# A windowed-attention block on one core: new order of stages, score weights of 49 columns, long matmuls in two 64-column halves, first MLP layer in f16

## The reference

```
xw   = windows of 7x7 pixels (64 per image), 49 tokens of 96 channels
xn   = layernorm(xw) * g + b
q,k,v = split(xn @ qkv_w.T + qkv_b)            # 12 heads of 8
attn = softmax(q * 8**-0.5 @ k.T + bias[head]) # 49 x 49
x1   = x + (attn @ v) @ proj_w.T + proj_b
c    = depthwise 3x3 convolution of x1, then batch norm (fixed statistics)
h    = gelu(c @ w1.T + b1)                     # 384 hidden channels, exact gelu
out  = c + (h @ w2.T + b2)
```

## Time and profile before

| | us |
|---|---|
| median of three runs | 3758.8 |
| lowest and highest | 3752.88, 3760.82 |
| the profiled execution | 3757.64 |
| its span, first to last instruction | 3755.8 |
| TensorE busy | 3535.0 (94%) |
| ScalarE busy | 3101.7 (83%) |
| VectorE busy | 2937.8 (78%) |
| GpSimd busy | 1133.5 (30%) |

### The profile page before, as it was taken

How to read it: one execution, slowest core, us unless ns; L and a number is a source line. 1 busy time by engine, 2 the same in 40 slices (tenths; PEclk the granted TensorE clock), 3 DMA queues, 4 the chain that set the end, 5 groups by cost and what they waited for, 6 DMA issues and landing times.

```text
span 3755.8 us, 189287 instructions
## 1 busy us (share of the span) xinstructions
PE 3535.0 (94%) x83724; PEld 2303.3 (61%) x83724; DVE 2937.8 (78%) x5155; ACT 3101.7 (83%) x5123; POOL 1133.5 (30%) x1550
## 2 busy tenths in 40 slices
PE   4999999999999999999999999999999999999998
PEld 2666666666666666666666666666666666666664
DVE  4778787877878778787877878787787878778786
ACT  2788888888888888888888888888888888888886
POOL 2232332323233232333233233232323323232332
PEclk9999999999999999999999999999999999999999
DMA  1232332323233232322323233232323223232321
GB/s 46 82 91 85 89 89 84 91 84 91 85 88 90 84 91 84 91 87 87 88 86 91 85 90 90 84 91 84 91 85 89 88 85 92 83 91 84 90 89 47
DMA packets 269476, 321.37 MB, mean 86 GB/s; under 512 B 55124, under 2 KB 252181, under 8 KB 268663
## 3 DMA queue, kind: packets, MB, share of 16 engines
q1 hardware_dynamic: 235894, 232.12, 21.6%
q0 software_dynamic: 32768, 77.14, 6.2%
HBM read 39.35 MB, written 38.54 MB: 21 GB/s over the span
## 4 chain that ended last, share of the span: by engine, by line
PE 76%; ACT 12%; DVE 7%; issue 4%; SPq 1%; DMA 0%; POOL 0%; POOLq 0%; DVEq 0%; ACTq 0%
PE a_ps L438 13%; PE sm_ps L322 10%; PE o_ps L339 8%; PE a_ps L357 6%; PE a_ps L430 6%; DVE mx L673 5%; PE st_ps L307 5%; PE d_ps L349 5%; PE b_ps L430 4%; PE d_ps L430 4%; ACT sq L561 4%; PE b_ps L280 4%; ACT sq L563 4%; ACT sq L557 3%; PE b_ps L282 2%
## 5 line engine op out<-in xcount | busy, mean ns | idle before, releaser
L695 DVE SCALAR_TENSOR_TENSOR s<-ximg,cols,s 96x392 f32<-96x392 f32 x2048 | 1260.0, 615 | 20.8 <-POOL s L597 2.9
L673 DVE TENSOR_REDUCE mx<-sm_ps 128x12 f16<-128x588 f32 x1024 | 780.9, 763 | 435.4 <-PE sm_ps L322 435.4
L597 POOL TENSOR_TENSOR s<-ximg,cols 96x392 f32<-96x392 f32 x256 | 215.6, 842 | 2384.7 <-DVE y L726 2384.7
L499 ACT ACTIVATE p<-st_ps 128x588 f32<-128x588 f32 x1024 | 669.5, 654 | 130.7 <-PE st_ps L307 126.6
L322 PEld LDWEIGHTS sm_ps<-k_all,q_all 127*64 127x64 f16 x24576 | 472.5, 113 | 315.6 <-issue 210.5
L438 PE MATMUL a_ps<-g,w_s 128*96 128x392 f32 x1536 | 602.2, 501 | 0.0
L604 POOL DMA_DIRECT2D ox<-o_sb x1024 | 580.8, 570 | 47.9 <-issue 31.8
L322 PE MATMUL sm_ps<-k_all,q_all 127*64 127x49 f16 x24576 | 580.5, 192 | 7.9 <-DMA q_all<-ql 6.4
L307 PEld LDWEIGHTS st_ps<-q_all,k_all 128*64 128x64 f16 x24576 | 476.1, 113 | 151.8 <-issue 147.9
L307 PE MATMUL st_ps<-q_all,k_all 128*64 128x49 f16 x24576 | 562.3, 191 | 0.0
L339 PE MATMUL o_ps<-p,v 128*32 128x49 f32 x24576 | 428.1, 211 | 131.0 <-DVE mx L673 129.5
(11 more groups left out here) (98 smaller groups left out, 5539.7 us busy)
## 6 DMA issues: line engine op xcount, KB each, us to landing
ox<-o_sb POOLq DMA_DIRECT2D x1024, 73.5 KB, 2.6
k_all<-kh SPq DMA_DIRECT2D x512, 96.0 KB
q_all<-qh SPq DMA_DIRECT2D x512, 96.0 KB
x_sb<-in_x SPq DMA_DIRECT2D x256, 147.0 KB, 2.4
out<-y SPq DMA_DIRECT2D x256, 147.0 KB, 2.9
k_all<-kl SPq DMA_DIRECT2D x256, 96.0 KB
q_all<-ql SPq DMA_DIRECT2D x256, 96.0 KB
q_all<-mxt SPq DMA_DIRECT2D x256, 12.0 KB, 2.0
```

Of the source, the lines that this page charges most:

```text
L499: af(p32[:, q, :, :].rearrange("p (b h) n -> p b h n", b=2), st_ps[:, :, 0:HALF].rearrange("p b (h n) -> p b h n", n=TOK), ACT.Exp).then_i ...
L673: v.tensor_reduce(mx[:, (st[1] - lag) % 2, :, p].rearrange("p (b h) -> p b h", b=2), sm_ps[:, :, 0:HALF].rearrange("p b (h n) -> p b h n", ...
L695: v.scalar_tensor_tensor(acc, image_rows(st, lag, k // 3, k % 3), cw_c[:, k:k + 1], acc, ALU.mult, ALU.add)\
```

## The change

It does the following.

- TensorE's long matmuls go through `wide`, which issues two matmuls with 64 columns of weights each, into partitions 0 to 63 and 64 to 127. The weights of `centred`, `variance`, `projection` and `second` are padded with zeros to 128 columns; those of queries and keys take the neighbouring columns. `values` does the same. The score matmuls take 49 columns of weights, not 64; the unused rows of the score banks are cleared once in the setup.
- The first MLP layer: w1 is split into two f16 parts (times 256), and s2 into sh (GpSimd, `image_high`) and sl (GpSimd, `image_low`), three f16 passes (`wide_three`), Gelu with scale 1/256.
- The values go to v32 in one VectorE multiplication (`values_out`) with a mask column, 128 x 768 elements, for both windows of a pair; ScalarE's half is gone.
- Each of four groups of scores, maxima, exps, value products, taps and hidden parts has a semaphore of its own, with one count per chunk. `free` lists who used a bank last.
- The banks are dealt anew: centred, the second layer and hidden 0 in b_ps; variance, queries, projection and hidden 2 in a_ps; keys, values and hidden 1 in d_ps.
- The order of a step and several lags are new on every engine, as the loops at the end of the diff's parts show. STEPS is 267.

```diff
-        x_in = sems("x_in", 4)
+        x_in = sems("x_in", 8)
...
+            for s in range(STEPS):
+                term(k_all, 2, kh, kh_done, s - 4)
+                term(q_all, 2, ql, ql_done, s - 4)
+                store(s - 11)
+                load(s)
+                maximum_row(s - 5)
+                first_term(k_all, 1, kl, kl_done, s - 3)
+                term(q_all, 0, qh, qh_done, s - 3)
+                term(k_all, 0, kh, kh_done, s - 3)
+                term(q_all, 1, qh, qh_done, s - 3)
...
+            def wide(o, w, m, start=True, stop=True):
+
+                for h in range(2):
+                    last = mm(o[64 * h:64 * h + 64], w[:, 64 * h:64 * h + 64], m, start=start, stop=stop)
+                return last
+
+            def wide_three(o, sh, sl, mh, ml):
+
+                wide(o, sh, mh, stop=False)
+                wide(o, sh, ml, start=False, stop=False)
+                return wide(o, sl, mh, start=False)
...
-                        last = mm(st_ps[64 * w:64 * w + 64, h // HH, c0:c0 + TOK], k_all[:, r, h, n:n + WP],
-                                  q_all[:, r, h, n:n + TOK], start=True, stop=True)
+                        last = mm(st_ps[64 * w:64 * w + TOK, h // HH, c0:c0 + TOK], k_all[:, r, h, n:n + TOK],
+                                  q_all[:, r, h, n:n + TOK], start=True, stop=True)
...
+                free(pe, (y_done, c-8), (g_done[0], c-8), (xn_done, c-1))
+                at = c % CPI * CT
+                wide(b_ps[0:128, 0:CT], center[:, :], x_sb[:, at:at + CT]).then_inc(xc_done, 1)
...
+                if k == 1:
+                    wait(pe, sl_done, c)
+                if k == 0:
+                    free(pe, (xn_done, c+7), (y_done, c-1), (g_done[0], c-1))
+                elif k == 1:
+                    free(pe, (v32_done, c+5), (kl_done, c+6), (g_done[1], c-1))
+                elif k == 2:
+                    free(pe, (sum_done, c+2), (lnv_done, c+7), (ql_done, c+6), (g_done[2], c-1))
+                wide_three(hidden_ps[k][:, 0:CT], w1_h[:, k * 128:(k + 1) * 128], w1_l[:, k * 128:(k + 1) * 128], sh[:, :], sl[:, :]).then_inc(hid_done[k], 1)
...
+            for s in range(STEPS):
+                max_scores(s - 2, 0)
+                hidden(s - 8, 2)
+                exp_scores(s - 4, 3)
+                values_times_p(s - 4, 0)
+                second(s - 8, 1)
+                max_scores(s - 2, 1)
+                keys(s - 1)
+                queries(s - 1)
+                second(s - 8, 0)
+                second(s - 8, 2)
+                exp_scores(s - 3, 0)
+                values_times_p(s - 4, 2)
+                values_times_p(s - 4, 3)
+                max_scores(s - 2, 2)
+                centred(s)
+                values(s - 2)
+                exp_scores(s - 3, 1)
+                variance(s)
+                max_scores(s - 2, 3)
+                exp_scores(s - 3, 2)
+                projection(s - 5)
+                values_times_p(s - 3, 1)
+                maxima_rows(s - 2)
+                hidden(s - 7, 1)
+                hidden(s - 7, 0)
...
+            for s in range(STEPS):
+                inverses(s - 5)
+                exp(s - 4, 3)
+                outputs(s - 4, 0)
+                query_high(s - 1)
+                exp(s - 3, 0)
+                outputs(s - 4, 1)
+                square(s)
+                exp(s - 3, 1)
+                log_variance(s)
+                root(s)
+                exp(s - 3, 2)
+                act.preload_act_table_set("gelu_and_others")
+                gelu(s - 7, 1)
+                input_high(s)
+                gelu(s - 7, 0)
+                gelu(s - 7, 2)
+                act.preload_act_table_set("natural_log_exp_and_others")
+                log_sums(s - 4)
+                key_high(s)
...
+            def image_high(c):
+
+                if not real(c):
+                    return
+                wait(pool, tap_done[8], c)
+                wait(pool, hid_done[2], c - 1)
+                pool.sem_inc(turn, 1)
+                nc.gpsimd.tensor_copy(sh[:, :], s2[0:C, c % 2, :]).then_inc(sh_done, 1)
...
+                tt(sl[:, :], s2[0:C, c % 2, :], sh[:, :], ALU.subtract).then_inc(sl_done, 1)
+
+            for s in range(STEPS):
+                image_high(s - 7)
+                image_low(s - 7)
+                first_tap(s - 6)
+                input_low(s)
+                to_channels(s - 3)
...
+                v.tensor_tensor(v32[:, c % 2, :, :, :].rearrange("p h n (d x) -> p (h n d) x", x=4)[:, :, 0:2],
+                                d_ps[:, 0:NP * C].unsqueeze(2).broadcast_to([128, NP * C, 2]),
+                                half_c[:, :].unsqueeze(1).broadcast_to([128, NP * C, 2]), ALU.mult).then_inc(v32_done, 1)
...
+            for s in range(STEPS):
+                tap(s - 7, 3)
+                tap(s - 7, 4)
+                tap(s - 7, 5)
+                maxima(s - 2, 1)
+                key_low(s - 1)
+                normalise(s - 5)
+                tap(s - 7, 6)
+                block_out(s - 8)
+                tap(s - 7, 7)
+                query_low(s - 1)
+                maxima(s - 2, 2)
+                tap(s - 7, 8)
+                values_out(s - 2)
+                maxima(s - 2, 3)
+                input_normal(s)
+                image_sum(s - 5)
+                maxima_out(s - 2)
+                tap(s - 6, 1)
+                tap(s - 6, 2)
+                maxima(s - 1, 0)
```

More of the change, by code:

```diff
@@ L269, in _, with load, term @@
-            run(sp, step)
+            def load(c):
+                if not real(c):
+                    return
+                wait(sp, sum_done, c - CPI)
+                at = c % CPI * CT
+                sp.dma_start(x_sb[:, at:at + CT], dram_rows(x, c)).then_inc(x_in[c % 8], 16)
+            def term(t, n, part, done, c):
+                if not real(c):
+                    return
+                wait(sp, done, c)
+                sp.dma_start(t[n:TERMS:4, c % 4, :, :], part[:, c % 2, :]).then_inc(exp_in[c % 4], 16)
@@ new lines, in first_term, with maximum_row @@
+            def first_term(t, n, part, done, c):
+                if real(c):
+                    wait(sp, sm_done[3], c - 4)
+                    wait(sp, st_done[3], c - 4)
+                    term(t, n, part, done, c)
+            def maximum_row(c):
+                if not real(c):
+                    return
+                wait(sp, mxt_out, c)
+                sp.dma_start(q_all[MAXROW:MAXROW + 1, c % 4, :, :].rearrange("p h (n c) -> p (h n) c", c=2 * WP),
+                             mxt[:, c % 2, :]).then_inc(row_in[c % 2], 16)
@@ L606, in _, with input_low, first_tap @@
-            run(pool, step)
+            def input_low(c):
+                if not real(c):
+                    return
+                wait(pool, xh_done, c)
+                tt(xl[0:C, c % 2, :, 0:TOK], xn[:, :, :], xh[0:C, c % 2, :, 0:TOK], ALU.subtract).then_inc(xl_done, 1)
+            def first_tap(c):
+                if not real(c):
+                    return
+                wait(pool, sum_done, c)
+                wait(pool, y_done, c - 2)
+                tt(s2[0:C, c % 2, :].rearrange("c (r q) -> c r q", q=SIDE), image_rows(c, 0, 0),
+                   cw_c[:, 0:1].unsqueeze(2).broadcast_to([C, WS, SIDE]), ALU.mult).then_inc(tap_done[0], 1)
@@ L777 @@
         low[row:row + n] = -1.0
+    half = np.zeros((128, 2), np.float32)
+    for w in range(2):
+        half[64 * w:64 * w + TOK, w] = 1 / UP
     col = lambda v: a(v).reshape(C, 1)
@@ L793 @@
         "eye": np.eye(128, dtype=np.float32),
-        "low": low,
+        "low": low, "half": half,
     }
```

664 lines of the change are left out of this document (279 added, 385 removed).

## The result

The changed kernel takes 3697.1 us (median of 4 runs, 3688.9 to 3708.0) beside 3756.7 for the kernel before: ratio 0.984, 95% interval 0.981 to 0.988. It is faster by 1.6%, where 3317 us (-11.7%) was forecast and the range ended at 3510. The executions profiled took 3757.6 us before and 3688.9 us after.

A forecast was written before the change was run, and what follows sets the result against it. TensorE bounded the old kernel; afterwards loops crossing engines would. The larger loop, 12.4 us, plus 0.1 for margins gives 12.5 per step; 248 x 12.5 + 215 + 2 = 3317 us, range 3170 to 3510.

The forecast's parts named there:

- the sum of 11.5 us: TensorE's work per step after the change, without waits, with halves running side by side: 11.5 us.
- no 0.09: Expected sign on TensorE: the 0.09 us per change of weight-column shape vanishes between scores and long layers.
- rival B: Crossing loops longer, by slower GpSimd or VectorE work, no 49-column gain, or late second halves: 13.1 us, 3466 us; chance 0.21.
- rival C: On TensorE, f32 halves run one after the other: 15.4 us per step, 4036 us, slower than before; chance 0.05.
- ScalarE and VectorE: Busy time per step on these engines: ScalarE 11.25 us with two table loads, VectorE 11.5 with values_out at 1.0.
- GpSimd: mechanism: GpSimd's four DMA issues stand before its copy (0.85 us) and remainder (1.3), delaying hidden 1 on TensorE by 0.8.
- Loop 2: Chain from TensorE through outputs, GpSimd's DMA issues, copy and remainder to hidden 1 and the next step: 12.3 us.
- The DMAs: this step: SP's six term transfers: last issued at 9.3 us, landed some 2.5 later, before the next step at 12.3.
- rival D: No gain in time: another wait, the six term DMAs above all, lands 1.8 us later; 14.27, 3757 us; chance 0.03.
- The third theory: From the experiments, not the prediction: several loops without slack turn any jitter into time; called the weaker one.

The follow-up runs named there:

- e11: Changed kernel with the transfer order of e5 and score groups of 12 matmuls with a doubled moving operand (odd heads get even heads' scores): 3297.1 us.
- e5: Changed kernel with its six term transfers in another order on SyncE, both transfers of kh first: 3562.6 us, ratio 0.948.
- e12: Changed kernel with the order of e5, values in whole 128-column weights, and max_scores(2) moved between second(0) and second(2): 3437.3 us, ratio 0.914.
- e9: Changed kernel with the order of e5 and TensorE's blocks spread so that short ones don't crowd, VectorE's order following: 3595.5 us, ratio 0.957.
- e6: Changed kernel with score groups of 12 matmuls with a doubled moving operand, and without the six term transfers and the waits on them: 3279.1 us.
- e3: Changed kernel with its long matmuls undivided, one of 128 weight columns instead of two of 64: 3757.3 us, ratio 0.999 to the kernel before.
- e7: Changed kernel with one TensorE block, second(2), moved from before exp_scores(0) to between values_times_p(2) and values_times_p(3): 3696.1 us, ratio 0.984.
- e8: Changed kernel with both the transfer order of e5 and the moved block of e7: 3661.5 us, ratio 0.974.

## Why the prediction was wrong

**TensorE, the sum of 11.5 us: right, as far as the blocks go.** Added up from their starts, without waits, the blocks of a step of the changed kernel come to about 11.7. Halves run side by side (0.69 for an f32 layer, 0.17 for a pass), a score group takes 0.33 to 0.34 (0.31 forecast), no 0.09 stands between scores and long layers, a layer of three passes takes about 0.5. The square starts 0.90 us after the first matmul of centring, 0.21 behind the block's 0.69: the second half is not late, so that part of rival B and rival C fall. With both causes cured (e11) the step is 12.2 us in the median, with 0.5 taken off by its shorter score stream; 12.4 was forecast with the whole one.

**ScalarE and VectorE: right.** Groups of the changed kernel, by line and shape (busy us, mean ns of one, idle before):

```profile
L560 ACT ACT_TABLE_LOAD x267 | 342.6, 1283 | 4.8
L565 ACT ACT_TABLE_LOAD x267 | 342.6, 1283 | 4.7
...
L758 DVE TENSOR_TENSOR v<-d_ps,half_c 128x768 f32<-128x768 f32 x256 | 243.5, 951 | 64.1 <-PE d_ps L253 64.0
...
L623 POOL TENSOR_TENSOR sl<-s,sh 96x392 f16<-96x392 f32 x256 | 236.5, 924 | 21.7
L616 POOL CAST sh<-s 96x392 f16<-96x392 f32 x256 | 134.1, 524 | 36.8 <-DVE s L731 36.6
```

From 200 to 3200 us ScalarE is busy for 11.1 us a step and VectorE for 11.8 (11.25 and 11.5 forecast). values_out takes 0.95 (1.0), and the two table loads are all. ScalarE idles 0.69 before the square in the step shown (0.7 forecast).

**GpSimd: mechanism right, sizes wrong both ways.** The copy takes 0.52 (0.85 taken), the remainder 0.92 (1.3 taken): 0.7 less. But the first of the four DMA issues starts 0.69 us after `outputs` ends (0.05 taken), in the changed kernel and in e5, e11 and e12 alike: 0.6 more. In e12 it is 6.3 us from the end of value matmul 3 to the next step (1802.53 to 1808.81), as forecast, and that is partly luck. Loop 2 is the bound of e12 (its chain is 59% TensorE and 24% GpSimd), with a step of 12.7 us in the median, 12.9 in the mean, and 0.4 to 0.5 of wait before hidden 1; 12.3 and 0.8 were forecast, with an order that has no max_scores(2) of 0.33 us in this place. A mean of 12.94 instead of 12.5 over 248 steps is 109 of the 120 us by which e12 still lies above 3317.

**The DMAs: this step failed, by its size.** The prediction said: "the last is out at 9.3 and down some 2.5 later (x takes 2.4), before the next step at 12.3. The margin of 0.5 is thin." In the 101 steps of the changed kernel (200 to 3400 us) in which TensorE waited for ql, kh starts 3.8 us after max_scores(0) began, the first transfer 1.2 later, the last issue 4.0 after that: 9.0, 0.3 better than forecast. But from there to the next max_scores(0) it is 4.7 us, not 2.5. The four add up to 13.7, and that is the mean step there. In the other 129 steps the issue gaps come to 1.2 us each, and the step is 14.1. One transfer that lands late among six was given the time of a lone one of another shape. Others are later too: out<-y lands 4.3 us after its issue (2.9 before), q_all<-mxt 2.9 (2.0). The mechanism stood in the text as rival D, with a chance of 0.03 and 14.27 us.

An extreme case in the changed kernel: SP issues the transfer, and TensorE goes on 6.26 us later.

```profile
1627.02 0.67 SPq L211 DMA_DIRECT2D q_all<-ql  x1
```

```profile
1633.28 0.76 PE L312 MATMUL sm_ps<-k_all,q_all 127*49 127x49 f16 x24 [2.72 <-DMA q_all<-ql]
```

**The instruction supply: a term put at nothing.** The prediction priced the added matmuls and weight loads by what they stream, and never as instructions to be fetched. A step grew from 654 instructions to 742 (83,724 and 94,988 matmuls over 256 chunks, as many loads), and at the same time the short blocks were put together: two score groups, two value blocks and the 24 short matmuls of values stand around one long layer, 248 instructions in 2.6 us (1804.24 to 1806.88). In the kernel before, the densest 256 took 3.77 us, with long layers and the half microsecond of waiting for mx between the short blocks. The size: 192 us of gaps in the changed kernel, and in e9, which has the instructions of e5 (210 us) in another order, 3. e11 against e5 is 266 us, of which up to 8 x 0.06 x 256 = 123 are the shorter score groups. With both terms eased (and values in whole matmuls again), e12 takes 3437 us, inside the range of 3170 to 3510.

The Trainium skill (Runtime: NRT & Kernel Launch, section Instruction fetch mechanics) says that instructions come in blocks of 16 KiB, 256 of them, fetched ahead in sequence, and that this is hidden because an engine dispatches slower than its store is filled. The packets here are as it says. That it is hidden holds for the kernel before and not for the changed one, with 176 gaps of over 0.3 us at the ends of such blocks.

**The clock.** Its mean granted value was 0.996 before and is 0.971 now; over 200 to 3200 us it is 1.00 and 0.98. Some long stalls are followed by a fall to the lower of its two levels, 1.2 GHz: 20 of the 44 gaps of over 1.5 us from 200 to 3200 us, soon after. Two stretches of the changed kernel (length, busy by engine, clock), the second of them just behind a pause of TensorE of 1.90 us that ended at 1826.75:

```profile
1800.00:1826.50 26.50, 23.08 (x696) 15.71 (x688) 22.45 (x38) 20.89 (x36) 9.84 (x15) 1.00 0.33 94
...
1827.70:1829.60 1.90, 1.90 (x38) 1.31 (x35) 1.86 (x4) 1.26 (x3) 1.01 (x1) 0.50 0.04 9
```

A mean of 0.971 for two levels of 1 and 0.5 is 5.8% of the span at the lower one, 214 us, against 0.8%, 30 us, before. As work at the lower level takes at most twice as long (a score group 0.59 us there, 1827.97 to 1828.56, for 0.33), this is an estimate of at most 92 us on top of the stalls. It was not taken apart further; e6, without either stall, still has 0.984.

The third theory may have a part: where several loops are within 0.5 us of each other, a stall of one engine is not made up later. That is not shown; no experiment here measured it by itself.

## What to carry to other kernels

Count TensorE's instructions over time, not only what they stream. Where 256 in a row (matmuls and weight loads both count) took less than about 3.5 us here, it stopped in the middle of a block (in e3 rarely); spread or merge the short ones. To tell such a stop from a wait for data, see whether the gaps sit at the same place modulo 256. For a transfer that closes a loop, take its landing from the queue it shares, not from a lone transfer, and issue first what is ready first: a mere order was worth 135 us here. A block that is moved must not overtake what it waits for (e7, e8).

## Not expected of the hardware

A gap in the middle of a group of score matmuls, put down to "issue", ended 2.5 us after the start of an instruction packet and 1.4 us after its end (medians of the 176 of the changed kernel; nine in ten of the first lie between 2.2 and 2.9); packets take about 1.1 us in both kernels. Term transfers go out on SP 0.72 us apart, but 40 of 1,376 issues (200 to 3400 us) took over 1.0 us, up to 2.0. A score group of 24 matmuls with 49 moving columns takes 0.33 us, one of 12 with 98 moving columns 0.27: half the weight loads save a fifth.
